# One bias product per chunk of values, and the recurrence's gates among the first units of maxima

## The reference, cut to what matters

```python
# xn = layernorm(x)
hg = einsum('bld,ed->ble', xn, W)              # recurrence: hidden, gate
hidden, gate = hg[..., :D], hg[..., D:]
# h_t = sigmoid(-gate) * h_(t-1) + sigmoid(gate) * g(hidden), written with logs
x = conv(xn) + conv_b                          # three taps
qkv = x @ wqkv.T + bqkv                        # 16 heads of 8
q, k, v = split(qkv, 3)
attn = softmax(q @ k.T / sqrt(8))              # 2048 x 2048 for each head
ctx = attn @ v
```

## Time and profile before

| | us |
|---|---|
| median of three timed runs | 1295.79 (1295.3 to 1296.53) |
| profiled execution, its own time | 1292.26 |
| its span, from the first to the last instruction | 1290.5 |
| busy in that span: PE / DVE / ACT / POOL | 1166.9 / 921.9 / 833.0 / 344.5 |

### The profile page before, as it was taken

The page is one execution under the profiler, slowest core; times in us unless marked ns, Lnnn a source line. Parts: engine busy times, 40 slices in busy tenths (PEclk is TensorE's granted clock), DMA queues, the critical chain, the costliest instruction groups (busy, mean ns, idle before and its releaser), DMA issues. The chain is left out here.

```text
span 1290.5 us, 19528 instructions
## 1 busy us (share of the span) xinstructions
PE 1166.9 (90%) x6050; PEld 454.4 (35%) x6051; DVE 921.9 (71%) x1477; ACT 833.0 (65%) x1545; POOL 344.5 (27%) x855
## 2 busy tenths in 40 slices
PE   6969999999999999999998699999997574999995
PEld 2512222222222222222222454444443433666664
DVE  3289999999999999999996333233338762566665
ACT  2548888898888889889888343333334430465662
POOL 0356662243222432123121200000000165022322
PEclk9759999999999999999999789899999696999995
DMA  3313321032101321110111392000000001011103
GB/s 99 119 30 69 94 70 53 28 96 60 36 28 43 88 52 36 35 62 29 37 35 34 129 407 66 16 17 24 24 1 0 1 27 54 22 41 37 43 26 114
DMA packets 63948, 73.64 MB, mean 57 GB/s; under 512 B 28386, under 2 KB 43882, under 8 KB 63346
## 3 DMA queue, kind: packets, MB, share of 16 engines
q1 hardware_dynamic: 52346, 55.49, 13.2%
q0 software_dynamic: 10592, 15.76, 4.9%
q10 hardware_dynamic: 926, 1.34, 0.3%
HBM read 42.41 MB, written 30.10 MB: 56 GB/s over the span
## 5 line engine op out<-in xcount | busy, mean ns | idle before, releaser
L1065 DVE TENSOR_REDUCE mx<-PS 128x1 f32<-128x1024 f32 x512 | 593.8, 1212 | 35.5 <-PE PS L1479 25.2
L1494 PE MATMUL PS<-big 59*128 59x512 bf16 x1024 | 295.3, 387 | 9.0 <-ACT xnT L819 1.8
L1479 PE MATMUL PS<-big 56*128 56x512 bf16 x1024 | 204.0, 390 | 21.6 <-DVE mx L1065 9.3
L819 ACT ACTIVATE ctx_sb<-PS 128x512 f32<-128x512 f32 x344 | 187.8, 604 | 29.8 <-PE PS L1494 29.8
L819 ACT ACTIVATE xn_rows<-PS 128x512 f32<-128x512 f32 x340 | 185.7, 605 | 23.1 <-PE PS L1494 22.9
L819 ACT ACTIVATE xnT<-PS 128x512 f32<-128x512 f32 x340 | 185.7, 605 | 20.7 <-PE PS L1494 20.7
L1142 DVE TENSOR_TENSOR ctx_sb<-xcT,PS 128x512 f32<-128x512 f32 x128 | 87.9, 687 | 142.3 <-PE PS L1604 74.4
L1494 PEld LDWEIGHTS PS<-big 59*128 59x128 bf16 x1024 | 73.0, 93 | 324.8 <-ACT ctx_sb L819 98.1
L859 ACT ACTIVATE xcT<-PS,col_sb 128x512 f32<-128x512 f32 x128 | 87.8, 687 | 140.7 <-PE PS L1596 124.6
L642 POOL TENSOR_SCALAR neg_m<-mx 128x1 f32<-128x1 f32 x256 | 68.9, 287 | 378.2 <-DVE mx L1065 378.2
L1596 PE MATMUL PS<-xnT,w_bufs 128*128 128x512 f32 x256 | 134.5, 608 | 0.2 <-ACT xcT L859 0.2
(11 more groups left out here) (240 smaller groups left out, 1203.4 us busy)
## 6 DMA issues: line engine op xcount, KB each, us to landing
o_dram<-o_sum SPq DMA_DIRECT2D x64, 256.0 KB, 2.0
big<-in_w_all SPq DMA_DIRECT2D x4, 3072.0 KB, 26.1
big<-parts_dram POOLq DMA_DIRECT2D x42, 128.0 KB, 4.6
w_bufs<-o_dram SPq DMA_DIRECT2D x4, 1024.0 KB, 5.5
w_bufs<-in_w SPq DMA_DIRECT2D x16, 256.0 KB, 2.7
xg_dram<-v_cols POOLq DMA_DIRECT2D x4, 780.0 KB, 12.2
late<-xg_dram SPq DMA_DIRECT2D x48, 65.0 KB, 1.8
big<-parts_dram SPq DMA_DIRECT2D x58, 48.0 KB
```

Of the source, the lines that this page charges most:

```text
L819: nc.scalar.activation(probs[i % SLOTS][:, r, :], PS[:, SB + n % SLOTS, :], ACT.Exp, scale=DH ** -0.5).then_inc(exp_done, 1)
L1065: v.tensor_reduce(mx[:, b % 2, 2 * u + half:2 * u + half + 1], PS[:, MB + 2 * half:MB + 2 * half + 2, :].rearrange("p b n -> p (b n)"), AX ...
L1479: mm = pe.matmul(PS[:, MB + 2 * half + k, :], q_all[rows_of, h, t * P:(t + 1) * P], k_all[rows_of, h, half * CH:(half + 1) * CH], start=Tr ...
L1494: pe.matmul(PS[:, SB + n % SLOTS, :], k_all[rows_of, h, at:at + P], q_all[rows_of, h, qc * CH:(qc + 1) * CH], start=True, stop=True).then_ ...
```

## The change

The bias row is repeated four times (512 numbers, so the row's DMA grows), and one product of 512 columns puts it into the whole bank ahead of the four tiles' products. GD products move to banks 7, 0, 1, 2 in turn. Two of them come before the first unit of maxima, one after each of units 0 to 5. PE waits for the values' chunks to be taken out before the first unit, and for all results only behind unit 7. On POOL two `mix_gates` come ahead of `split_maxima(0)` and two behind it.

```diff
-for _name, _w in (("bv", P), ("ln2_g", P), ("ln2_b", P),
+for _name, _w in (("bv", CH), ("ln2_g", P), ("ln2_b", P),
...
+        GD_BANKS = (7, 0, 1, 2)
...
-            for c in range(C - 1):
-                mix_gates(c)
+            mix_gates(0)
+            mix_gates(1)
             for b in range(BLOCKS):
                 split_maxima(b)
                 if b == 0:
-                    mix_gates(C - 1)
+                    mix_gates(2)
+                    mix_gates(3)
                     pool.wait_ge(gru_mix, C)
                     pool.wait_ge(q_parts_out, 16 * PARTS)
...
-                nc.scalar.activation(sig_h[:, at], PS[:, bank_of(n), :], ACT.Relu, scale=-1.0).then_inc(relu_set, 1)
-                nc.scalar.activation(sT[:, at], PS[:, bank_of(n), :], ACT.Relu).then_inc(proj_act, 1)
+                bank = PS[:, GD_BANKS[2 * c % C], :]
+                nc.scalar.activation(sig_h[:, at], bank, ACT.Relu, scale=-1.0).then_inc(relu_set, 1)
+                nc.scalar.activation(sT[:, at], bank, ACT.Relu).then_inc(proj_act, 1)
...
             def values(c):
                 def mms(bank):
+                    pe.matmul(bank, ones_row[:, :], row("bv")[0:1, :], start=True, stop=False)
                     for i in range(TC):
                         t = c * TC + i
-                        pe.matmul(bank[:, i * P:(i + 1) * P], xcT[:, t * P:(t + 1) * P],
-                                  mat("qkv")[:, 2 * P:3 * P], start=True, stop=False)
-                        last = pe.matmul(bank[:, i * P:(i + 1) * P], ones_row[:, :], row("bv")[0:1, :],
-                                         start=False, stop=True)
+                        last = pe.matmul(bank[:, i * P:(i + 1) * P], xcT[:, t * P:(t + 1) * P],
+                                         mat("qkv")[:, 2 * P:3 * P], start=False, stop=(i == TC - 1))
                     return last
                 return mms
...
-            for c in range(2 * C):
-                if c < C:
-                    pe.wait_ge(proj_act, PROJ.n("Q", c))
-                    pe.wait_ge(rest_set, C + c + 1)
+            def gates(i):
+                if i == 0:
+                    pe.wait_ge(proj_act, PROJ.n("Q", C - 1))
+                    pe.wait_ge(rest_set, 2 * C)
+                elif i < C:
+                    pe.wait_ge(proj_act, PROJ.n("V", i - 1))
                 else:
-                    pe.wait_ge(proj_act, PROJ.n("V", c - C))
-                at = c % 2 * P
-                first("GD", c, project(mat("gru")[:, at:at + P], xnT[:, 1:N + 1])(c // 2))
+                    pe.wait_ge(proj_act, PROJ.n("GD", i - C))
+                at = i % 2 * P
+                project(mat("gru")[:, at:at + P], xnT[:, 1:N + 1])(i // 2)(PS[:, GD_BANKS[i % C], :]).then_inc(proj_mm, 1)
...
-            pe.wait_ge(proj_act, PROJ.total)
-            pe.wait_ge(identb_set, 1)
-            pe.wait_ge(ones_in, 32)
+            gates(0)
+            gates(1)
+            pe.wait_ge(proj_act, PROJ.n("V", C - 1))
             for g in range(LEAD):
                 maxima_half(g, 0)
                 maxima_half(g, 1)
+                if g + 2 < 2 * C:
+                    gates(g + 2)
+            pe.wait_ge(proj_act, PROJ.total)
+            pe.wait_ge(ones_in, 32)
...
-    rows = {"bv": bqkv[2], 
+    rows = {"bv": np.tile(bqkv[2], TC),
```

More of the change, by code:

```diff
@@ L794, in _ @@
                 act.wait_ge(proj_mm, n)
-                nc.scalar.activation(sig_h[:, at], PS[:, bank_of(n), :], ACT.Relu, scale=-1.0).then_inc(relu_set, 1)
-                nc.scalar.activation(sT[:, at], PS[:, bank_of(n), :], ACT.Relu).then_inc(proj_act, 1)
+                bank = PS[:, GD_BANKS[2 * c % C], :]
+                nc.scalar.activation(sig_h[:, at], bank, ACT.Relu, scale=-1.0).then_inc(relu_set, 1)
+                nc.scalar.activation(sT[:, at], bank, ACT.Relu).then_inc(proj_act, 1)
                 n = PROJ.n("GD", 2 * c + 1)
                 act.wait_ge(proj_mm, n)
-                nc.scalar.activation(gate_z[:, at], PS[:, bank_of(n), :], ACT.Sigmoid).then_inc(gates_set, 1)
-                nc.scalar.activation(gate_c[:, at], PS[:, bank_of(n), :], ACT.Sigmoid, scale=-1.0).then_inc(proj_act, 1)
+                bank = PS[:, GD_BANKS[(2 * c + 1) % C], :]
+                nc.scalar.activation(gate_z[:, at], bank, ACT.Sigmoid).then_inc(gates_set, 1)
+                nc.scalar.activation(gate_c[:, at], bank, ACT.Sigmoid, scale=-1.0).then_inc(proj_act, 1)
                 act.wait_ge(relu_set, c + 1)
```

## The result

The changed kernel takes 1285.97 us (median of four runs, 1285.74 to 1287.7) against 1295.55 of the kernel before (four runs, 1294.2 to 1296.53): a ratio of 0.993, 95% interval 0.9912 to 0.9947. That is 9.6 us less, where 11.1 were forecast. The profiled execution took 1286.12, its span 1284.3. Two executions of later runs stand far from the rest, 1314.21 in gates_only and 3587.16 in head3_early, and are in no ratio. Lines in the changed file stand 1 to 9 further down than before (the reduce is L1069, maxima are L1484, scores L1499).

What follows compares the result with a forecast made beforehand. DVE and PE, both full through the attention, were taken to bind the time to unit 8's start: 12.1 us earlier, less 1.0 for ACT, is 11.1 off 1295.79, giving 1284.7 us; range 1278.5 to 1291.

Steps and rivals of the forecast that it cites:

- The bound: Attention, 104 to 690 us: DVE and PE both full, so it moves with PE's unit 8, at 85.64 before.
- Values: PE's values products: 2.2 us a new chunk against 3.3, ending at 44.1, or about 47 if the clock falls.
- First unit: PE's first unit of maxima: at 48.4 against 67.44, 19 us earlier, with ends of 47 and 50.2.
- The term for the loads: Head 0's queries on POOL: last issued at 45.0, landed 3.4 us later at 48.4, holding the first unit.
- Units and last gate: Units 0 to 7 with gate products between: last gate product at 61.5 (full clock) to 66.0 (half), 63.7 taken.
- What is late next: Head 2's 12 loads on ACT behind the last gate: 8.25 us of issue, unit 8 at 73.5, 12.1 us earlier.
- the landing: Head 2's last load, ahead of unit 8: lands some 1.5 us behind its issue.
- Behind unit 8: ACT's way to the first exponential: ends at about 75.8, scores ready at 74.5, PE waits about 1 us.
- rival 2: Before unit 8: head 2's loads don't hold it, unit 8 at 68 to 70, 17 us gained, 1278.8; chance 0.08.
- Rival 3: Whole kernel: nothing changes, 1295.8, since an unseen chain sets the attention's end; chance 0.05.
- rival 1: PE at half the clock all along: unit 8 at 77.6, 8.0 us gained, 1 lost on ACT, 1288.8; chance 0.20.
- Rival 4: Behind unit 8: clock stays at half, 1.98 us more per step with values; 50 us would give 1306.7; chance 0.05.

Runs made afterwards that it cites:

- gates_only: The changed kernel with the old values (a 128-column bias product to each tile), so the gates' move alone: 1292.6 us, ratio 0.9981.
- head3_early: The changed kernel with head 3's 12 loads issued by POOL and SP right behind head 1's, head 2's left on ACT: 1285.08 us, ratio 0.9919.
- full_row_bias: The changed kernel with the bias product over all 128 rows (ones of 1/128) in place of one row: 1286.55 us, ratio 0.9933.
- loads_early: The changed kernel with head 2's 12 loads taken off ACT, queries issued by POOL and keys by SP behind head 1's: 1279.92 us, ratio 0.9882.
- mixes_spread: The changed kernel with heads 2 and 3 loaded early by POOL and SP, and only one mix ahead of POOL's first split: 1278.93 us, ratio 0.9878.
- after_again: The changed kernel unaltered, run again beside head3_early on the same chip: 1285.55 us, ratio 0.9922.
- values_only: The kernel before with only the new values and long bias row, gates' order, banks and waits as before: 1286.57 us, ratio 0.9937.

## Why the prediction was right, point by point

- **The bound was right.** The attention hardly catches up, and the time goes with unit 8 (table).
- **Values.** 2.2 us a chunk were forecast, 2.14 measured; the switch of operand shapes was the cause named for it, and full_row_bias shows it: with 128 rows in both products a chunk takes 37.91 - 36.16 = 1.75, so two switches cost 0.39 (forecast: 0.36). The clock fell in the profiled execution, the branch that was forecast to end at 47 (46.69).
- **First unit.** 48.4 was taken, held by head 0's loads; it came at 50.25, held by the two gate products at half the clock, the branch that was forecast to end at 50.2. The term for the loads was too small as well. Its 3.4 us is the median of four small loads; the one that ends head 0's queries took longer, in the kernel before (DMA issues from 44.73 to 45.43) and in the change (4.2, landed at 49.3):

```profile
big<-parts_dram POOLq DMA_DIRECT2D x1, 8.0 KB, 4.9
```

- **Units and last gate.** 63.7 forecast, 63.8 measured. That is luck in part, two errors that cancel: the first unit came 1.9 later, and the units went at the pace forecast for the full clock (2.26 against 2.28) in all but the first, where a mixture of both clocks was taken.
- **What is late next.** Head 2's loads, named as the new wait, were it. The issue took 8.29 (8.25 forecast). **The step that failed in size is the landing**: 1.5 us behind the last issue were read from a stretch in which nothing else was moved, and 4.34 passed. In the new place POOL and SP load head 3 in the same stretch, which goes with about 1.6 of it in head3_early; the rest stays open. Unit 8 came at 76.46, not 73.5: 9.2 us earlier, not 12.1.
- **Behind unit 8.** The 1 us that ACT was to lose (75.8 - 74.5, its own times, give 1.3) did not appear: the first exponential came 1.05 behind unit 8 (77.51 - 76.46), as before, because unit 8 was later than ACT's table load (76.0). The attention was 1.3 longer all the same; PE's first later waits for maxima's rows and DVE's small waits lie there, and no run took them apart.
- **The sum.** Forecast 11.1; unit 8 gave 9.2: the landing was 2.8 longer than its term, and the 1.0 for ACT did not come, two errors that cancel in part. The two profiled executions differ by 6.1, the medians by 9.6: the way behind the attention was 1.7 longer in the profile after, inside the 2.8 by which it varies, and the profiled execution of before, 1292.26, lies under all four timed runs of its kernel.
- **Rivals.** Of rival 2 (loads do not hold unit 8) the change shows the contrary, and loads_early what it would have been: unit 8 at 68.8 (68 to 70 forecast), 1279.92 us (1278.8 forecast). Rival 3, no change, lies outside the interval of the ratio. Of rival 1 the clock at half came in part: among the values and from unit 8 on, not among the units. The Trainium skill's rule ("TensorE: Matmul & The Clock Gate", section "HAM oscillation — how this bites in real kernels") that a wait between bursts leaves the next burst at half agrees with the 8.66 us pause and the stretch at 0.50 behind it. But the pause is not shown to be the cause: the clock fell as it began, and mixes_spread, without it, has 0.51 in the same stretch. Rival 4, a clock that stays down, did not come: it was up again 12 us behind unit 8.
- What the prediction did not see: the gates' part is worth next to nothing by itself (1.9 us), and with the values changed it adds nothing that can be measured (1285.97 and 1285.55 against 1286.57). It was forecast to bring the first unit forward, and did, while it put the gates' end, and with it head 2's loads, as late as the values alone leave unit 8.

## What to carry to other kernels

Before a stage is started earlier, list what the stage needs at its third and fourth piece, and on which queue that stands: work put between the first pieces delays everything that was queued behind that work. Loads whose data are ready should be issued by a queue with nothing to wait for, ahead of the stage; here this was worth 6 us, and the gates' move by itself 1.9. A landing time read in a quiet stretch, or as a median of several loads, was too small here for the load that a stage waited for (1.5 against 4.34 us, 3.4 against 4.2).

## What the runs showed that was not expected

The moment at which the clock falls among the values differs between executions of the same code. The change's values took 46.69 - 35.33 = 11.36 us in one profile and, in after_again, from 36.10 to 49.23, 13.1; values_only's, the same instructions, 8.46 with the clock at 1.00 throughout. PE was busy without a pause in all three. That is a spread of 4.7 us from one stage. Between the two profiles of the change it carries through: values 1.8 longer and a start 0.8 later put unit 8 2.6 and the end of the span 2.7 later. The timed runs of the unaltered change beside head3_early lie 5.1 apart (1283.65 to 1288.79); that the clock among the values is behind all of it is not shown.

A float32 product of 128 columns takes 0.24 us between others of its shape and 0.42 beside products with one row, at the same clock. The weight loads (PEld) show what differs. First full_row_bias, then the change:

```profile
36.59 0.19 PEld L1426 LDWEIGHTS PS<-mat_sb,xcT 128*128 128x128 f32 x1 [0.24 <-issue]
```

```profile
36.38 0.97 PEld L1426 LDWEIGHTS PS<-mat_sb,xcT 128*128 128x128 f32 x8 [0.76 <-issue]
```

Behind a bias product of 128 rows (36.16) the tiles' first weight load starts 0.43 ahead of the product that needs it (37.02), while the bias product runs; behind one of a single row (35.33) it starts only with the tiles' products, at 36.38. A chunk takes 1.75 us in the one case and 2.14 in the other. The Trainium skill, "TensorE: Matmul & The Clock Gate", section "Part 3: Packing small matmuls — row/col tiling", lists weight loads as overlapping with running matmuls only where the row groups differ, and names the background weight buffer beside that. The list by itself does not fit here: 128 rows behind 128 rows overlap, one row and 128 rows in turn do not.
